# Attention stages: row-halved stacks and paired score matmuls, one block further apart

## The reference

```python
q = _split_heads(query @ wq_k + wq_b, H)
k = _split_heads(key_in @ wk_k + wk_b, H)      # 77 context rows
v = _split_heads(value @ wv_k + wv_b, H)
logits = jnp.einsum('bhqd,bhkd->bhqk', q, k) / jnp.sqrt(jnp.asarray(dh, q.dtype))
attn = jax.nn.softmax(logits + neg[:, None, :, :], axis=-1) * group_prob[:, None, :, :]
out = jnp.einsum('bhqk,bhkd->bhqd', attn, v)
out = out.transpose(0, 2, 1, 3).reshape(query.shape[0], -1, H * dh)
return out @ wo_k + wo_b
```

## Time and profile before

| | us |
|---|---|
| median of three runs | 5596.02 (5586.29 to 5598.56) |
| the profiled execution | 5577.15, span 5575.1 |
| first to last start of a score matmul, x0 | 2659.7 to 3250.5 |
| the same, f | 3331.2 to 3825.0 |
| the same, a | 4276.9 to 4825.2 |
| the same, x1 | 4891.1 to 5312.1 |
| busy over the span: TensorE, VectorE, ScalarE, GpSimd | 72%, 81%, 50%, 56% |

### The profile page before, as it was taken

One profiled execution on the slowest core, in us unless ns is written; L12 is line 12 of the kernel. 1 busy time (PEld: TensorE's weight loads), 2 busy tenths in 40 slices (PEclk: granted clock), 3 DMA queues, 4 the chain that ended last, 5 costly groups with the idle time before them and its releaser, 6 DMA issues. The chain is left out here.

```text
span 5575.1 us, 103824 instructions
## 1 busy us (share of the span) xinstructions
PE 4029.1 (72%) x29177; PEld 2314.7 (42%) x29180; DVE 4512.3 (81%) x8773; ACT 2779.2 (50%) x6405; POOL 3140.3 (56%) x3422
## 2 busy tenths in 40 slices
PE   5777778777777787774777748887283888689943
PEld 2333233332333333332455536666283666456621
DVE  5999999999999999996898877776246777667778
ACT  3545555455555554552677734445374455345434
POOL 6877777777777777775565643324544222233302
PEclk8999989988998999987888869997696888799965
DMA  2111111011101110111545526666115555366511
GB/s 82 65 52 48 67 67 67 36 65 67 66 33 67 67 67 36 65 65 28 100 87 86 94 55 107 112 110 166 48 60 118 96 101 95 67 114 119 104 40 30
DMA packets 320172, 420.38 MB, mean 75 GB/s; under 512 B 40000, under 2 KB 301712, under 8 KB 309136
## 3 DMA queue, kind: packets, MB, share of 16 engines
q1 hardware_dynamic: 315536, 408.35, 31.4%
q0 software_dynamic: 4352, 8.95, 0.5%
HBM read 307.65 MB, written 109.58 MB: 75 GB/s over the span
## 5 line engine op out<-in xcount | busy, mean ns | idle before, releaser
L2184 POOL TENSOR_TENSOR m_h<-m_dtu,m_Bb 128x512 f32<-128x512 f32 x1024 | 1589.5, 1582 | 229.3 <-PE bank L1819 223.1
L1819 PE MATMUL bank<-m_h,ident 128*128 128x512 f32 x2048 | 1211.3, 682 | 500.1 <-DVE m_h L2083 487.2
L1819 PEld LDWEIGHTS bank<-m_h,ident 128*128 128x128 f32 x2048 | 362.0, 206 | 1163.3 <-DVE m_h L2083 1014.9
L2077 DVE TENSOR_TENSOR_SCAN m_h<-m_dA,m_h 128x512 f32<-128x512 f32 x512 | 750.5, 1466 | 6.3 <-DVE m_sz L2010 6.3
L2083 DVE TENSOR_TENSOR m_h<-m_h,bank 128x512 f32<-128x512 f32 x1024 | 674.2, 659 | 5.2 <-issue 3.4
L2077 DVE TENSOR_TENSOR_SCAN m_h<-bank,m_h 128x512 f32<-128x512 f32 x512 | 621.3, 1214 | 27.9 <-DVE m_sz L2010 11.9
L1966 ACT ACTIVATE bank<-m_dt,m_A 128x512 f32<-128x512 f32 x512 | 352.3, 688 | 495.6 <-DVE m_h L2077 435.5
L1966 ACT ACTIVATE m_dA<-m_dt,m_A 128x512 f32<-128x512 f32 x512 | 367.2, 717 | 429.4 <-DVE m_h L2077 425.6
L516 ACT ACTIVATE x_sm<-x_sm,x_nm 128x77 f32<-128x77 f32 x1024 | 353.5, 349 | 113.3 <-DVE x_nm L679 112.9
L861 POOL TENSOR_TENSOR x_sm<-x_sm,x_gp 128x308 f32<-128x308 f32 x256 | 219.5, 860 | 132.3 <-ACT x_sm L516 132.3
L377 PE MATMUL bank<-ident,x_sm 128*77 128x128 f32 x1024 | 195.9, 322 | 134.5 <-DVE x_pT L702 121.5
(11 more groups left out here) (422 smaller groups left out, 10560.0 us busy)
## 6 DMA issues: line engine op xcount, KB each, us to landing
m_Bb<-m_B SPq DMA_DIRECT2D x32, 4096.0 KB, 12.0
x_Ks<-x_k_parts SPq DMA_DIRECT2D x32, 462.0 KB
x_q_parts<-x_qp SPq DMA_DIRECT2D x32, 384.0 KB, 4.0
x_Qs<-x_q_parts SPq DMA_DIRECT2D x32, 384.0 KB
f_Ks<-f_k_parts SPq DMA_DIRECT2D x16, 768.0 KB
a_Ks<-a_k_parts SPq DMA_DIRECT2D x16, 768.0 KB
x_xp<-x_stage SPq DMA_DIRECT2D x32, 256.0 KB
x_Qs<-x_q_parts SPq DMA_DIRECT2D x32, 256.0 KB
```

Of the source, the lines that this page charges most:

```text
L1819: pe.matmul(banks[4 + c], ident[:], h[:, k % RING, :], start=(s == 0), stop=(s == NS - 1)).then_inc(s_ya.sem, 1)
L2077: v.tensor_tensor_scan(h[:, k % RING, :], decays[k % AHEAD], h[:, k % RING, :], 0.0, ALU.mult, ALU.add).then_inc(s_h.sem, 1)
L2184: pool.tensor_tensor(h[:, k % RING, :], dtu[:, d, c, :], Bb[:, d, s, :], ALU.mult).then_inc(s_dB.sem, 1)
```

## The change

- The stacks lie in two 64-row halves: blocks 0 and 1 of a group in partitions 0 to 47, blocks 2 and 3 in 64 to 111. `Qs` and `Ks` are half as wide, and their matmuls use only 48 partitions, so the compiled program places them in a 64-row tile of the array at row 0 or 64. The memsets of `Qs`, `Ks` and `pT` go.
- Each store of parts and each fill is cut in two, one per half; the first half is filled before the store of an older group's result, and each half has its own semaphore.
- In f, a and x1, `scores` of block b alternates with the transposed scores of block b-2 (which always lie in the other half) head by head; the four `sel` matmuls follow together, over all 128 partitions, with `nmT` now holding four blocks. `shifted` goes.
- `LATER` is 1 there: values, output and residual come one block later. `turn_max` moves from c=0 to c=1, the copy of the maxima on VectorE from c=0 to c=2. The pipeline drains one block later.
- The projection of v moves from slot 3 to 4 of a group, and VectorE's evacuation of it to slot 8.
- In x0 only the stacks, stores, fills and the slots of v change.

The core of the diff:

```diff
-    TAIL = 6
+    LATER = 1 if gate is None else 0
+    TAIL = 6 + LATER
+    HB = GB // 2
@@ rms: the slots of v (the other two cases: "v": 3 -> 4, later 3 -> 4)
-        slot = {"x": -8, "qt": -7, "kt": -6, "qn": -3, "kn": -2, "v": 3}
-        later = {"v": 1, "high": 0, "middle": 1, "squares": 0, "root": 1, "norm": 2}
+        slot = {"x": -8, "qt": -7, "kt": -6, "qn": -3, "kn": -2, "v": 4}
+        later = {"v": 4, "high": 0, "middle": 1, "squares": 0, "root": 1, "norm": 2}
@@
-        Qs = sb("Qs", [P, 2, H, GT], BF16)
-        Ks = sb("Ks", [P, 2, H, kt], BF16)
+        Qs = sb("Qs", [P, 2, H, HB * S], BF16)
+        Ks = sb("Ks", [P, 2, H, HB * sk], BF16)
-        nmT = sb("nmT", [P, 2, S], BF16)
+        nmT = sb("nmT", [P, GB, S], BF16)
+        def rows(q):
+            lo = 64 * (q // HB)
+            return slice(lo, lo + ROWS)
@@ sync: a turn
                         save_parts(g + 1, 1 - l)
+                        load_gate(g + 1, 1 - l)
+                        fill_stack(g + 1, 1 - l, 0)
                     if not first:
                         store(g - 2, l)
                     if not (last and l):
-                        load_gate(g + 1, 1 - l)
-                        fill_stack(g + 1, 1 - l)
+                        fill_stack(g + 1, 1 - l, 1)
                     residual(g, l)
@@ tensor
+                if then:
+                    pe.wait_ge(s_nmT.sem, s_nmT.at(b - 1))
+                    pe.wait_ge(s_e.sem, s_e.at(b - 2, c + 1 - 2))
                 for h in range(4):
                     hh = 4 * c + h
-                    ins = pe.matmul(bankS[c % 2][:, h * sk:(h + 1) * sk], Qs[:, l, hh, q * S:(q + 1) * S],
-                                    Ks[:, l, hh, q * sk:(q + 1) * sk], start=True, stop=True)
-                ins.then_inc(s_S.sem, 1)
+                    if now:
+                        ins = pe.matmul(bankS[c % 2][:, h * sk:(h + 1) * sk], Qs[rows(q), l, hh, cols(q, S)],
+                                        Ks[rows(q), l, hh, cols(q, sk)], start=True, stop=True)
+                        if h == 3:
+                            ins.then_inc(s_S.sem, 1)
+                    if then:
+                        pe.matmul(bankT[c % 2][0:sk, h * S:(h + 1) * S], Ks[rows(tq), tl, hh, cols(tq, sk)],
+                                  Qs[rows(tq), tl, hh, cols(tq, S)], start=(h == 0), stop=False)
+                if then:
+                    for h in range(4):
+                        ins = pe.matmul(bankT[c % 2][0:sk, h * S:(h + 1) * S], sel[:, 4 * c + h, 0:sk], nmT[:, tq, :],
+                                        start=False, stop=(h == 3))
+                    ins.then_inc(s_st.sem, 1)
@@ tensor: turn_max and out
-                pe.wait_ge(s_r.sem, s_r.at(b - 3))
+                pe.wait_ge(s_r.sem, s_r.at(b - 4))
-                    pe.wait_ge(s_nmT.sem, s_nmT.at(min(b + 4, B) if isinstance(b, int) else b + 4))
+                    pe.wait_ge(s_nmT.sem, s_nmT.at(min(b + 5, B) if isinstance(b, int) else b + 5))
@@ vector
-            dve.memset(Ks[:], 0.0).then_inc(s_zero.sem, 1)
             if gate is None:
                 dve.memset(nmT[:], 0.0).then_inc(s_zero.sem, 1)
-            if sk < P:
-                dve.memset(pT[:], 0.0).then_inc(s_zero.sem, 1)
-                if c == 0 and live(1) and gate is None:
+                if c == 2 and live(1) and gate is None:
                     maxima_rows(v, ch, b - 1, (lb - 1) % 8)
@@ gpsimd
-            pool.memset(Qs[:], 0.0).then_inc(s_zero.sem, 1)
```

More of the change, by code:

```diff
@@ L168, in attention @@
         s_mid = sem("mid_ready", 2); s_lo = sem("lo_ready", 2)
-        s_ps = sem("parts_stored", 16 * (PARTS + 1)); s_stk = [sem(f"stack_loaded{l}", 16 * (PARTS + 1)) for l in range(2)]
+        s_ps = sem("parts_stored", 32 * (PARTS + 1)); s_stk = [[sem(f"stack_loaded{l}{half}", 16 * (PARTS + 1)) for half in range(2)] for l in range(2)]
         s_ln = sem("front_var", 1); s_lp = sem("front_pow", 1); s_xn = sem("front_norm", 1)
@@ L195, in columns, with cols @@
             return t[:, 4 * c:4 * c + 4, u * VC + lo:u * VC + lo + n]
+        def rows(q):
+            lo = 64 * (q // HB)
+            return slice(lo, lo + ROWS)
+        def cols(q, n):
+            return slice(q % HB * n, (q % HB + 1) * n)
         def heads(t):
@@ L287, in _ @@
             save_parts(0, 0)
-            sp.wait_ge(s_zero.sem, NZ)
-            fill_stack(0, 0)
+            for half in range(2):
+                fill_stack(0, 0, half)
             turn(0, first=True)
@@ L358, in turn_max @@
                              identb[:]).then_inc(s_T.sem, 1)
[L360 to L370, removed]
             def turn_weights(b, lb, c):
@@ L416, in step @@
                 b = 8 * i + lb
-                if live(0):
-                    scores(i, lb, c)
+                scores(i, lb, c, live(0), gate is None and live(2))
                 if gate is not None:
@@ L421, in step @@
                         turn_weights(b - 1, (lb - 1) % 8, c)
[L422 to L427, removed]
-                    shifted(b - 1, (lb - 1) % 8, c - 1)
-                if live(2):
-                    values(b - 2, (lb - 2) % 8, c)
-                if c == 1 and live(3):
-                    turn_out(b - 3)
-                if c == out_at and live(4):
-                    out(b - 4)
-                if c == 3 and live(3):
-                    turn_back(b - 3)
+                elif c == 1 and live(1):
+                    turn_max(b - 1, (lb - 1) % 8)
+                n = 2 + LATER
+                if live(n):
+                    values(b - n, (lb - n) % 8, c)
+                if c == 1 and live(n + 1):
+                    turn_out(b - n - 1)
+                if c == out_at and live(n + 2):
+                    out(b - n - 2)
+                if c == 3 and live(n + 1):
+                    turn_back(b - n - 1)
             def slots(i, lb, c, last):
@@ L869, in step @@
                         gated(b, lb, c - 2, (i + 1) * 16)
-                if c == 1 and lb % GB == 0 and bo is not None and live(1):
-                    t, l = (i, 0) if lb else (i - 1, 1)
+                if c == 1 and lb % GB == LATER and bo is not None and live(1 + LATER):
+                    t, l = (i, 0) if lb >= GB else (i - 1, 1)
                     pool.wait_ge(s_xr[l].sem, (t + 1) * 16)
@@ L2629, in _ @@
                                pattern=[[-1, P]], channel_multiplier=1).then_inc(s, 1)
-            for part in range(3):
-                pool.affine_select(out=sel[:], in_=sel[:], compare_op=ALU.not_equal, fill=1.0, base=-part * H,
+            for n, lo in enumerate((0, H, 2 * H, 64, 64 + H, 64 + 2 * H)):
+                pool.affine_select(out=sel[:], in_=sel[:], compare_op=ALU.not_equal, fill=1.0, base=-lo,
                                    pattern=[[-1, H], [0, P]], channel_multiplier=1).then_inc(s, 1)
-                pool.wait_ge(s, 8 + part)
+                pool.wait_ge(s, 8 + n)
     return {"ident": ident, "identb": identb, "ones_row": ones_row, "sel": sel, "half_pow": half_pow}
```

108 lines of the change are left out of this document (60 added, 48 removed).

## The result

The changed kernel takes 5740.87 us in the median (5713.65 to 5760.38), the kernel before on the same chip 5591.66: a ratio of 1.0263 (95% interval 1.0209 to 1.0317). It is slower, by 149 us where 143 us less were forecast. The profiled execution took 5713.65 us (span 5711.6). The mean granted clock of its span is 0.802, of the one before 0.855, both as shares of 2.4 GHz; the clock records of both profiles hold only 1.2 and 2.4 GHz, so such a mean tells how long it stood at which.

The account below looks back on a forecast made before the run. VectorE was taken to bound x0; in f, a and x1 TensorE and VectorE hold each other up. f -50, a -45, x1 -24, x0 +8, drains +11, starts -43 sum to -143: 5596 to 5453 us, range 5375 to 5590.

Parts of the forecast that it names:

- rival of the four: VectorE takes over, 5522 (0.15); everything filled, 5369 (0.15); no overlap of pairs, 5602 (0.12); drains, 5645 (0.08).
- Part 1, pairs: Scores and transposed scores overlap in two row halves, 0.056 us a pair: -33 us each in f and a, -11 in x1.
- Part 2, distance: One more block of distance removes TensorE waits: f -17, a -25, x1 -13 us; new waits in a +13.
- The forecast of a wait at out in x1: Out projection shares bank 6 with VectorE's copy of the maxima: 0 to 0.3 us a block, inside the half taken.
- The wait for vS in a: TensorE's turn of x waits for a reduction and the values' evacuation: about 0.9 us a group, 15 groups, +13 us.
- Part 3, starts: Stage starts, without the Qs memset and with scores needing only half the stack: -43 us in all, bounds -29 and -50.
- Part 4, x0: In x0, without pairs, one extra change of shape a step, a third of 24 us landing: +8 us, 0 to 24.
- Slower: the drains: Rival: 64-row shape changes in four stages cost twice 0.093 us, losing 0.19 a step, 192 us: 5645; chance 0.08.
- drains at the ends: f, a and x1 drain one block later, 3.6 us of TensorE each: +11 us.

Follow-up runs that it names:

- order128: Changed kernel with the earlier 128-partition stacks, whole stores and fills, memsets and 128-partition values, keeping the new order: 5572 us, ratio 0.9961.
- rows65: Kernel before, scores and transposed scores over 65 partitions in all four stages, transposed four ahead of their sel matmuls: 5759 us, ratio 1.0289.
- rows48: Kernel before, scores and transposed scores over 48 partitions in a 64-row tile, transposed four ahead of sel: 6037 us, ratio 1.0837.
- k77: Kernel before, values' matmuls in x0 and x1 over 77 partitions instead of 128, pT not cleared: 5597 us, ratio 1.0030.
- after_v128: Changed kernel, values' matmuls of x0 and x1 over 128 partitions again, pT cleared at the start: 5616 us, ratio 1.0060.
- pairs64: Changed kernel, scores and transposed scores over the whole 64-row half (16 added rows hold zeros) in all four stages: 5618 us, ratio 1.0063.
- order128b: order128 with all four scores ahead of the transposed four, out in x1 at a block's last step, Qs memset on VectorE: 5504 us, ratio 0.9854.
- rows64: Kernel before, scores and transposed scores over 64 partitions, so a 64-row tile, transposed four ahead of sel: 5970 us, ratio 1.0693.
- unpaired: Changed kernel, a step's four scores put ahead of its four transposed scores in the program instead of alternating: 5792 us, ratio 1.0404.
- pairs64s: Changed kernel with full 64-row halves, x0 as before, x1's out at last step and values over 128, sel over one half: 5576 us, ratio 0.9969.

## Why the prediction was wrong, point by point

**The step that failed** is the one on which all terms of parts 1 and 4 rest: TensorE's prices were read at the clock of the kernel before, and the same clock was assumed after. The earlier trace rows show that it was not fixed (0.84 to 1.00 by stage). No rival of the four held a fall of the clock. It fell in all four stages (x0 0.84 to 0.64, f 0.92 to 0.83, a 0.88 to 0.74, x1 0.98 to 0.87), and at half the clock a step's matmuls cost 1.7 us instead of 1.0. order128 shows that the order had no part in it; rows65, rows48, k77 and after_v128 show what had: matmuls over fewer partitions, in the scores and in the values. Why the clock follows the partitions stays open.

**Part 1, pairs.** The mechanism was right to a hundredth: pairs each 0.055 us, 0.15 to sel, 0.33 from sel to the values with its drain. The -33 us each for f and a did not appear: f stayed at 495, where the same order over 128 rows gives 470. A saving of 0.13 us a step was paid with a clock of 0.83 instead of 0.94. Even over full halves f took 468 (pairs64), so no run shows the 33 us. A small slip: 0.59 to 0.54 us in the 256 steps of x1 is 13 us, not 11.

**Part 2, distance.** Right in direction for f and a, wrong for x1. order128, which has the order as changed, is 24 us shorter in f and 19 in a, beside -17 and -12 (-25 + 13), and 22 longer in x1, beside -13. order128b comes to 33, 26 and 13 us less, but with edits that the prediction did not have, so that it meets the 13 of x1 is luck. The forecast of a wait at out in x1 was 0 to 0.3 us a block; the changed kernel has 9.0 us in 50 blocks, 0.18. What it overlooked is what alternating does to x1: scores are complete later, 22 us in order128. The wait for vS in a was 25.6 us for 12 groups, 2.1 each, not 0.9; that is beyond the 1 us that the prediction had named as the sign of being wrong here. That out would wait for the copy in f too (29.3 us in 49 blocks) was not foreseen.

**Part 3, starts.** Right. From the first load of a stage's weights to its first scores, before and after: x0 49.5 and 39.8, f 58.7 and 40.7, a 45.7 and 39.6, x1 46.0 and 33.7 us, -46 in all beside -43. The cast that took 9.52 us takes 0.43:

```profile
4974.34 0.43 DVE L646 CAST x_qp<-x_qf 128x512 bf16<-128x512 f32 x1 [12.96 <-ACT x_qf L490]
```

But one item of the diff has no term: sel needs ones in its upper half too, six passes instead of three, ahead of everything. GpSimd, before and after, and SyncE's first load, before and after:

```profile
3.83 6.29 POOL L2632 TENSOR_SCALAR_AFFINE_SELECT sel<-sel 128x2048 bf16<-128x2048 bf16 x3
...
10.61 0.45 SPq L1672 DMA_DIRECT2D m_xg<-in_x  x1
```
```profile
3.84 12.73 POOL L2645 TENSOR_SCALAR_AFFINE_SELECT sel<-sel 128x2048 bf16<-128x2048 bf16 x6
...
17.05 0.45 SPq L1686 DMA_DIRECT2D m_xg<-in_x  x1
```

+6.4 us for the whole kernel.

**Part 4, x0.** Forecast +8, bounds 0 and 24; measured +73. Only a missed by more (forecast -45, measured +41). The bound came from one extra change of tile at a fixed clock, with VectorE as the cover. At 0.64 that cover was gone. The values over 77 partitions were costed at nothing, silently, and weigh most (after_v128: x0 51 us shorter, and the whole 125).

**The rivals.** "Slower: the drains" had the right side, and its figure of 0.19 us a step is what rows64 shows against rows65 (211 us in 1024 steps, 0.21). Its mechanism, a change that costs twice the 0.093, is wrong: it costs 0.10 at the full clock, and the rest came through the clock. The changed kernel went 96 us beyond its 5645. So it had the side by luck, not by its mechanism.

**The sum.** Stages +143 (x0 73, f 1, a 41, x1 28), starts -46, sel +6, drains at the ends about +5 each in a and x1 (3.6 forecast): 113 of the 136 us between the two profiled executions. The other 23 lie at the end of x0 (1.5), in the first stage, which ends 5 us later than sel explains, and between f's last scores and a's first load, with f's drain and the experts in it, which went from 406 to 423 us. From f's last to a's first scores the kernels above have 451 to 473 us without a pattern, those that leave f's order as before too, so most of that is no part of the change.

## What to carry to other kernels

Before a matmul is cut to fewer rows, look at the granted clock of its stage: where it stands below 1.00 or just at it, zero rows, which cost no time at a given clock, may be what holds the clock up. Read a saving on TensorE as time at a clock, not as time, and ask of every edit, the small ones too (77 partitions instead of 128), whether it leaves the array less to do. An order change and a cut of rows that come in one diff are worth timing apart: here the order gains 0.4% (1.5% with the three edits of order128b), and the rest loses 3.0%.

## What the runs showed of the hardware

- The granted clock of a stage fell with the number of partitions of its matmuls, at the same matmul count, tile and free size: 0.855 to 0.816 for the span when 63 of 128 rows, all zeros, were left out of the scores (rows65), 0.823 to 0.802 from 64 to 48 rows in pairs (pairs64 and the changed kernel), though not in x0 (0.62 and 0.64). The Trainium skill, TensorE: Matmul & The Clock Gate, Part 1, says that activity releases the half clock. That the engine's records were busier (402.62 of 450 us in x0 after, 344.17 before) while the clock fell from 0.84 to 0.67 shows that the busy share of a profile is not a measure of it. In this stretch of x1 in the changed kernel the clock stood at half from end to end, while the records of TensorE leave no gap:

```profile
5362.60:5407.00 44.40, 44.40 (x381) 26.79 (x380) 20.22 (x73) 14.51 (x30) 12.00 (x31) 0.50 0.41 70
```

- Two matmuls in different row halves start within 0.01 us of each other and share the array (f, changed kernel), even where three others stand between them in the program (unpaired). The Trainium skill, TensorE: Matmul & The Clock Gate, Part 3, gives 4 ns between row groups; the rows here agree to their 0.01.
- A change between a 64-row and a 128-row tile costs 0.10 us at 2.4 GHz (0.32 instead of 0.22, rows64 and rows65) and about 0.14 at 1.2 (0.25 from the last pair to sel, 0.11 without the change in pairs64s).
- Effects on the clock need not add up: the same edit of 51 zero rows was worth 18 us to x0 in the kernel before (k77) and 51 in the changed one (after_v128), in single executions.
